# Block turns by VectorE for four of sixteen attention units in a four-layer graph kernel

## The chip, the cores and the metric

The kernel runs on one core of one Trainium2 chip. The metric is the time of one execution on the device in microseconds. TensorE multiplies matrices and turns (transposes) tiles, VectorE and ScalarE work on rows, GpSimd does slower elementwise work, and SP (SyncE) only issues DMAs, one after the other, in the order of its program.

## The reference

Four graph layers run one behind the other on N = 4096 nodes with 128 features; `adj` is a dense 4096x4096 f32 matrix in which a zero means "no edge".

```
L0: msg = relu((adj @ x) @ W_msg.T + b);  x1 = layernorm(GRU(msg, x))
L1: x2 = layernorm(D^-1/2 (adj + I) D^-1/2 (x1 @ W) + b + x1)
L2: q, k, v = x2 @ Wq + bq, ...  (4 heads of 32)
    a = q k^T / sqrt(32), -inf where adj == 0;  alpha = softmax(a)
    out = alpha @ v;  r = x2 @ Ws + bs
    x3 = layernorm(beta * r + (1 - beta) * out + x2)
L3: xt = logmap(mobius(x3 @ W_h.T, bias));  y = layernorm(relu(...(adj @ xt)) + x3)
```

The layer norms and the residual sums are as the kernel's steps show them. All results are f32.

## The kernel before

**Layers 0, 1 and 3** multiply columns of `adj` from a ring of eight slots of 1 MB (`product`, L437; loads at L328 and L409) with a stationary operand, in eight chunks of 512 nodes. `stat_x` and `stat_s` hold the stationary tiles; `stat_s` is written by layer 0, read by layer 1, and its tiles are written again, chunk by chunk, for layer 3 by GpSimd's step `xt` (L1463).

**Layer 2, the attention,** is the stage that the change touches. Each of the 8 chunks has 4 row tiles of 128 nodes. The 4096 key nodes of a row tile are cut into 4 columns of 1024 (`BLOCK`), so a chunk has 16 columns. Two columns make a set, so a chunk has 8 sets. A set is worked off in 16 units (`UPS`) of 128 key nodes and a chunk has 128 units, also called places: every engine writes its instructions out in a loop over k = 0 to 127, and the constants say at which k something is done. Nothing but semaphores keeps the engines together.

- TensorE, `scores` (L541): at every even place, the scores of one head and one column ahead of time (two products of 512), `SCORE_LEAD` = 13 of these ahead, into two pairs of PSUM banks used in turn. It may not run more than two ahead of VectorE's masks.
- VectorE, `mask` (L1096): at every odd place, adds the mask, keeps the row minimum, and writes 128x1024 into `cols` (two sets deep, L226).
- ScalarE, `exponent` (L803): for one head of one set, a 128x2048 exp in place in `cols`, four a set, `EXP_LEAD` = 4 ahead, at the places in `EXP_PLACES`.
- TensorE, `turn_unit` (L573): for each unit, four 128x128 transposes (one a head) of `cols` into one of three PSUM banks (`TurnBanks`).
- The copy of a turned unit into SBUF, `turned[k % 8]`, by VectorE (43 of 128, L1115) or ScalarE (85 of 128, L810). The eight slots are pieces of `arena` (L227); slots 6 and 7 are stages 10 and 11.
- TensorE, `attend` (L584): four products of a turned unit with the values, summed in bank 7. They come in batches of four, `ATTEND_LAG` = 7 places behind: at places 3, 7, 11 and 15 of a set it attends four units, at place 11 units 4 to 7 of the set, at place 3 units 12 to 15 of the set ahead of it.
- GpSimd, `mask_bias` (L1353): turns two halves of an `adj` block (128x512 each) into a bf16 mask, column by column, `BIAS_LEAD` = 6 columns ahead. Between them stand the post steps of the chunk before (L1363 to L1467), and once a row tile the six small steps of `block_mix` (L1469).
- SP (L340 to L405): mask loads into two 128x512 buffers, each as soon as GpSimd has read what lay there; queries once a row tile; residuals and the store of x3 once a chunk. Then the ring loads of layer 3 follow in the same queue, the first four slots when the second to last set is turned, the others when the last one is.

## Time and profile before

| | us |
|---|---|
| median of 3 runs (least, most) | 1860.52 (1857.96, 1862.22) |
| the profiled execution's own time | 1859.99 |
| its span in the trace | 1858.3 |
| busy: TensorE matmul | 1805.1 |
| busy: TensorE weight load | 1215.9 |
| busy: VectorE | 1229.1 |
| busy: ScalarE | 983.0 |
| busy: GpSimd | 925.3 |

Matmuls are pipelined and their ends are modelled, so a TensorE that shows as busy is not thereby at its peak. The attention stage runs from about 600 to 1611 us of the span. PE is TensorE, PEld its weight load, DVE is VectorE, ACT is ScalarE, POOL is GpSimd, SPq is SP's queue of DMA issues.

### The profile page before, as it was taken

The numbers are of one execution on the slowest core, as the hardware profiler recorded it, in microseconds if no ns is written. First come the engines' busy times: TensorE is split into PE (matmuls) and PEld (weight loads), VectorE is DVE, ScalarE is ACT, GpSimd is POOL, SyncE is SP. The second block draws the span as 40 slices with busy tenths as digits, with TensorE's granted clock in tenths as the row PEclk, the third lists the DMA queues.
The fourth block names the chain that finished last, engine by engine and source line by source line (L and its number), as shares of the span: only waits on it lengthen the run. The fifth ranks groups of instructions, "written<-read, shape, count | busy, mean of one in ns | idle before, by whom it ended". The sixth has DMA issues, their size and how long they took to land.

```text
span 1858.3 us, 41304 instructions
## 1 busy us (share of the span) xinstructions
PE 1805.1 (97%) x15504; PEld 1215.9 (65%) x15504; DVE 1229.1 (66%) x2398; ACT 983.0 (53%) x1512; POOL 925.3 (50%) x981
## 2 busy tenths in 40 slices
PE   7999999999996999999999999999999999999996
PEld 3444444444444888888888888888888888644442
DVE  4777775122226888898888888888988889401322
ACT  0111110101004888888888888988888988501101
POOL 0111111111225756778788788787787886540211
PEclk9999999999997999999999999999999999999998
DMA  9867767799977322213222222232133231697781
GB/s 376 303 227 260 256 225 251 270 391 380 400 271 220 93 91 72 83 58 95 88 73 90 74 82 86 70 92 91 60 93 93 64 96 49 242 356 281 281 325 71
DMA packets 110305, 328.82 MB, mean 177 GB/s; under 512 B 13104, under 2 KB 31280, under 8 KB 85552
## 3 DMA queue, kind: packets, MB, share of 16 engines
q1 hardware_dynamic: 87552, 285.25, 43.9%
q10 hardware_dynamic: 20016, 32.78, 4.9%
q0 software_dynamic: 2560, 8.39, 1.6%
q8 instruction: 115, 1.88, 0.4%
q14 instruction: 62, 0.51, 0.1%
HBM read 299.11 MB, written 27.26 MB: 176 GB/s over the span
## 4 chain that ended last, share of the span: by engine, by line
PE 59%; issue 3%; ACT 2%; POOL 2%; DVE 1%; POOLq 0%; DVEq 0%; ACTq 0%
PE bank L580 21%; PE bank L553 13%; PE bank L594 13%; PE bank L446 11%; ACT arena L807 2%; POOL arena L1360 1%; DVE arena L1124 1%; PE bank L434 0%; ACT L858 0%; PE bank L622 0%; PE bank L690 0%; POOL small L1480 0%; ACT arena L819 0%; PE bank L602 0%; POOL small L1367 0%
## 5 line engine op out<-in xcount | busy, mean ns | idle before, releaser
L580 PE MATMUL bank<-ident,arena 128*128 128x128 f32 x4096 | 540.0, 274 | 5.4 <-ACT arena L807 2.4
L580 PEld LDWEIGHTS bank<-ident,arena 128*128 128x128 f32 x4096 | 478.1, 141 | 82.5 <-DVE arena L1124 7.7
L807 ACT ACTIVATE arena<-arena,small 128x2048 f32<-128x2048 f32 x256 | 512.5, 2002 | 0.1
L819 ACT ACTIVATE arena<-bank 128x512 f32<-128x512 f32 x680 | 382.4, 596 | 125.3 <-PE bank L580 123.0
L446 PE MATMUL bank<-arena,stat_s 128*128 128x512 f32 x1008 | 441.4, 595 | 2.1 <-issue 1.2
L553 PE MATMUL bank<-k,parts 128*128 128x512 f32 x1024 | 371.8, 445 | 13.3 <-DVE small L1109 7.0
L446 PEld LDWEIGHTS bank<-arena,stat_s 128*128 128x128 f32 x1008 | 190.2, 191 | 228.3 <-issue 226.9
L1124 DVE COPY arena<-bank 128x512 f32<-128x512 f32 x344 | 236.7, 688 | 73.3 <-PE bank L580 71.6
L1360 POOL TENSOR_SCALAR early<-arena 128x512 bf16<-128x512 f32 x128 | 246.3, 1925 | 68.9 <-DVE small L1109 26.7
L594 PE MATMUL bank<-arena,stat_x 128*32 128x128 f32 x8192 | 276.5, 276 | 0.0
L1360 POOL TENSOR_SCALAR arena<-arena 128x512 bf16<-128x512 f32 x128 | 247.2, 1931 | 40.5 <-DVE small L1109 19.8
L446 PE MATMUL bank<-arena,stat_x 128*128 128x512 f32 x512 | 229.2, 599 | 10.7 <-DMA arena<-adj_cols 8.5
L594 PEld LDWEIGHTS bank<-arena,stat_x 128*32 128x32 f32 x8192 | 208.1, 109 | 42.8 <-issue 42.8
L553 PEld LDWEIGHTS bank<-k,parts 128*128 128x128 f32 x1024 | 155.6, 191 | 68.0 <-issue 44.2
L446 PEld LDWEIGHTS bank<-arena,stat_x 128*128 128x128 f32 x512 | 96.4, 192 | 125.7 <-issue 125.4
L1109 DVE CUSTOM_DVE_ANT_0 arena<-bank,early,small 128x1024 f32<-128x1024 f32 x128 | 163.5, 1279 | 16.6 <-issue 9.3
L1109 DVE CUSTOM_DVE_ANT_0 arena<-bank,arena 128x1024 f32<-128x1024 f32 x128 | 155.9, 1219 | 26.2 <-PE bank L580 20.9
L1109 DVE CUSTOM_DVE_ANT_0 arena<-bank,arena,small 128x1024 f32<-128x1024 f32 x128 | 163.2, 1277 | 6.2 <-issue 5.2
L1109 DVE CUSTOM_DVE_ANT_0 arena<-bank,early 128x1024 f32<-128x1024 f32 x128 | 155.8, 1218 | 15.0 <-PE bank L553 7.8
L1305 POOL TENSOR_SCALAR small<-small 128x4 f32<-128x4 f32 x32 | 13.0, 407 | 251.5 <-DVE small L937 251.5
L1367 POOL TENSOR_TENSOR small<-small 128x4 f32<-128x4 f32 x160 | 78.8, 492 | 60.5 <-DVE small L1185 35.8
L1367 POOL TENSOR_TENSOR arena<-arena 128x512 f32<-128x512 f32 x64 | 76.3, 1192 | 36.4 <-ACT arena L848 20.7
(152 smaller groups left out, 1182.8 us busy)
## 6 DMA issues: line engine op xcount, KB each, us to landing
arena<-adj_cols SPq DMA_DIRECT2D x190, 1024.0 KB, 6.3
arena<-adj SPq DMA_DIRECT2D x256, 256.0 KB, 2.7
k_dram<-arena ACTq DMA_DIRECT2D x32, 256.0 KB, 6.7
q_dram<-arena ACTq DMA_DIRECT2D x32, 256.0 KB, 11.7
k<-k_dram POOLq DMA_DIRECT2D x32, 256.0 KB, 8.5
parts<-q_dram SPq DMA_DIRECT2D x128, 64.0 KB, 2.3
x_dram<-arena ACTq DMA_DIRECT2D x16, 256.0 KB, 3.6
arena<-x_dram ACTq DMA_DIRECT2D x16, 256.0 KB, 4.9
```

The lines of the kernel that those rows point to most:

```text
L446: mm_ = pe.matmul(bank[:, to, :], stat[:, jt, :], ring[:, s, j, :], start=(jt == 0), stop=(jt == TILES - 1))
L553: last = pe.matmul(bank[:, u + i, :], parts[:, t % 2, h * P:(h + 1) * P], k4[:, h, at_:at_ + CHUNK], start=True, stop=True)
L580: last = pe.transpose(bank[:, b_, h * P:(h + 1) * P], cols[:, st % SETS, h, u * P:(u + 1) * P], ident[:, :])
L594: last = pe.matmul(bank[h * C:(h + 1) * C, 7, st * P:(st + 1) * P], stat_x[:, k % UPT, h * C:(h + 1) * C], turned[k % TURNED][:, h * P:(h ...
L807: act.activation(cols[:, s_, h, :], cols[:, s_, h, :], ACT.Exp, bias=shift[:, t % 2, 1, i:i + 1], scale=-1.0, accum_out=blocksum[:, t % 2, ...
L819: act.activation(turned[k % TURNED], bank[:, TURN_BANKS.bank(("unit", k)), :], ACT.Copy).then_inc(unit_copied_act, 1)
L1109: dve.tensor_tensor_reduce(out=cols[:, s_, h, hi * BLOCK:(hi + 1) * BLOCK], in0=bank[:, 2 * (h % 2):2 * (h % 2) + 2, :].rearrange("p b n - ...
L1124: dve.tensor_copy(turned[k % TURNED], bank[:, TURN_BANKS.bank(("unit", k)), :]).then_inc(unit_copied_dve, 1)
L1305: step(c, "eps", pool.tensor_scalar(rstd, mean_var[:, :, 1], LN_EPS, None, ALU.add))
L1360: pool.tensor_scalar(maskbias[m % 4][:, e * HALF:(e + 1) * HALF], adj_in[e], 0.0, MASKED, ALU.is_equal, ALU.mult).then_inc(bias_ready, 1)
L1367: step(c, name, pool.tensor_tensor(out_, a, b, op))
```

## The change

Of the 16 units of a set, units 6, 7, 14 and 15 are no longer turned by TensorE. VectorE turns them from `cols` in 32x32 blocks (`turn_blocks`, one instruction over 128x512 a unit), at VectorE's places 0 and 1 (units 6 and 7) and 7 and 9 (units 14 and 15), into `pair_blocks`, which lies in the last eight tiles of `stat_s`. SP stores the pair to DRAM (512 KB, `store_pair`), waits for that, and loads it back (`load_pair`) in four DMAs of 128 KB, with runs of 1 KB, so that the four row blocks change places; the destination `pair_slot` is the two slots 6 and 7 taken together. The attend products of these units read `pair_slot` through a view with runs of 32. Loads wait until the pair that lay in the slots has been attended.

VectorE copies 12 units a chunk in place of 43, and ScalarE 84 in place of 85. Most exps change their place by one to three. SP's program is written out anew: in each column first the mask load of six columns on, then the pair store, then queries or the store of x3 where they are due, then the pair load. GpSimd waits for the last pair store ahead of the step `xt` that writes over `pair_blocks`.

```diff
+BLOCK_TURN_AT = {6: 0, 7: 1, 14: 7, 15: 9}
+PAIRS = ((6, 7), (14, 15))
-VECTOR_PLACES = (2, 5, 9, 12, 15)
-VECTOR_ALSO = (38, 58, 84, 87, 91, 93)
-VECTOR_NOT = (37, 57, 69)
-EXP_MOVED = {37: 38, 57: 58, 65: 66, 69: 71, 89: 88, 93: 94}
+VECTOR_PLACES = ()
+VECTOR_ALSO = (2, 19, 25, 58, 66, 82, 88, 89, 91, 98, 115, 123)
+VECTOR_NOT = ()
+EXP_MOVED = {1: 2, 5: 7, 13: 12, 17: 20, 21: 24, 25: 26, 29: 28, 37: 39, 45: 44, 49: 50, 57: 59, 61: 60, 65: 66, 69: 71, 73: 74, 77: 76, 85: 88, 93: 90, 97: 98, 101: 104, 105: 106, 109: 108, 113: 115, 117: 120, 121: 123, 125: 124}
+MASK_AHEAD = 6
...
+    pair_dram = nc.dram_tensor("pair_dram", [2, P, 2 * CHUNK], F32)
+        pair_slot = arena[:, RING + 10 * CHUNK:RING + 12 * CHUNK]
+        pair_blocks = stat_s[:, TILES - 2 * TPC:TILES, :].rearrange("p t f -> p (t f)")
+        def pair_tiles(ap):
+            return ap.rearrange("p (b u h n) -> p u h b n", b=P // C, u=2, h=H)
...
+            def store_pair(g):
+                i = pairs_until(g)
+                sp.wait_ge(blocks_turned, 2 * (i + 1))
+                if i >= 2:
+                    sp.wait_ge(pair_landed, 16 * (P // C) * (i - 1))
+                sp.dma_start(pair_dram[i % 2, :, :], pair_blocks).then_inc(pair_out, 16)
+            def load_pair(g):
+                i = pairs_until(g)
+                sp.wait_ge(pair_out, 16 * (i + 1))
+                if i == 0:
+                    sp.wait_ge(gcn_x2_out, 16 * CHUNKS)
+                if g + 1 >= TURNED:
+                    sp.wait_ge(unit_used, g + 1 - TURNED + 1)
+                for j in range(P // C):
+                    sp.dma_start(pair_slot[j * C:(j + 1) * C, :].rearrange("k (q n) -> k q n", q=P // C),
+                                 pair_dram[i % 2, :, j * 2 * P:(j + 1) * 2 * P].rearrange("(q k) n -> k q n", q=P // C)
+                                 ).then_inc(pair_landed, 16)
+            def attention_loads(c):
+                for st in range(SPC):
+                    for half_set in range(2):
+                        ahead = c * COLS + 2 * st + half_set + MASK_AHEAD
+                        if ahead < CHUNKS * COLS:
+                            load_mask(ahead // COLS, ahead % COLS, False)
+                        for pair in PAIRS:
+                            if pair[0] // UPB == half_set:
+                                store_pair(c * UPC + st * UPS + pair[0])
+                        if half_set == 1 and st % SETS == 1:
+                            ahead = c * TPC + st // SETS + 2
+                            if ahead < CHUNKS * TPC:
+                                load_queries(ahead // TPC, ahead % TPC, False)
+                        if half_set == 1 and st == 4 and c > 0:
+                            store_x3(c - 1)
+                        for pair in PAIRS:
+                            if pair[0] // UPB == half_set:
+                                load_pair(c * UPC + st * UPS + pair[0])
+                load_residuals(c)
...
+                if is_block_turned(k):
+                    pe.wait_ge(pair_landed, 16 * (P // C) * (pairs_until(c * UPC + k) + 1))
...
-                    turn_unit(c, k, first)
+                    if not is_block_turned(k):
+                        turn_unit(c, k, first)
...
+            def turn_blocks(c, k):
+                st, u = k // UPS, k % UPS
+                i = pairs_until(c * UPC + k)
+                dve.wait_ge(exp_ready, (c * SPC + st) * H + H)
+                if i > 0:
+                    dve.wait_ge(pair_out, 16 * i)
+                dve.transpose(pair_tiles(pair_blocks)[:, in_pair(k), :, :, :],
+                              cols[:, st % SETS, :, u * P:(u + 1) * P].rearrange("p h (j k) -> p h j k", j=P // C)
+                              ).then_inc(blocks_turned, 1)
...
+                    for u, place in BLOCK_TURN_AT.items():
+                        if k % UPS == place:
+                            turn_blocks(c, k - place + u)
```

## Rows read from the trace of the kernel before

**Rows 1.** The page, part 1: busy us, share of the span, instructions.
```profile
PE 1805.1 (97%) x15504; PEld 1215.9 (65%) x15504; DVE 1229.1 (66%) x2398; ACT 983.0 (53%) x1512; POOL 925.3 (50%) x981
```
**Rows 2.** The page, part 4: shares of the chain by line.
```profile
PE bank L580 21%; PE bank L553 13%; PE bank L594 13%; PE bank L446 11%; ACT arena L807 2%; POOL arena L1360 1%; DVE arena L1124 1%; PE bank L434 0%; ACT L858 0%; PE bank L622 0%; PE bank L690 0%; POOL small L1480 0%; ACT arena L819 0%; PE b
```
**Rows 3.** The chain in order of time: start us, us, what.
```profile
940.38 1.28 ACT L858
...
1452.59 1.28 ACT L858
```
**Rows 4.** Busy us by engine in seven chunk windows: one, then sum and mean.
```profile
928.70:1056.80 128.10, 127.26 (x1685) 105.81 (x1684) 112.86 (x207) 112.89 (x168) 101.48 (x107) 1.00 0.26 82
...
sum 896.70, PE 892.99 PEld 742.74 DVE 792.08 ACT 789.37 POOL 693.96; mean PE 127.57 PEld 106.11 DVE 113.15 ACT 112.77 POOL 99.14
```
**Rows 5.** TensorE in order of time: start us, us, line, tiles, count.
```profile
1111.48 0.73 PE L553 MATMUL bank<-k,parts 128*128 128x512 f32 x2
1112.06 1.03 PE L580 MATMUL bank<-ident,arena 128*128 128x128 f32 x8
1112.85 0.71 PE L553 MATMUL bank<-k,parts 128*128 128x512 f32 x2
1113.39 1.04 PE L580 MATMUL bank<-ident,arena 128*128 128x128 f32 x8
1114.36 1.08 PE L594 MATMUL bank<-arena,stat_x 128*32 128x128 f32 x32
```
**Rows 6.** Groups of one chunk, 928.6 to 1056.95: busy us, mean ns, idle before.
```profile
L594 PE MATMUL bank<-arena,stat_x 128*32 128x128 f32 x1024 | 34.6, 276 | 0.0
...
L1124 DVE COPY arena<-bank 128x512 f32<-128x512 f32 x43 | 29.6, 688 | 7.7 <-PE bank L580 7.4
...
L1189 DVE TENSOR_REDUCE small<-arena 128x4 f32<-128x512 f32 x1 | 0.7, 682 | 0.0
```
**Rows 7.** VectorE in order of time, the same stretch as rows 5.
```profile
1112.36 1.23 DVE L1109 CUSTOM_DVE_ANT_0 arena<-bank,arena 128x1024 f32<-128x1024 f32 x1
...
1113.51 0.69 DVE L1124 COPY arena<-bank 128x512 f32<-128x512 f32 x1
1114.12 1.22 DVE L1109 CUSTOM_DVE_ANT_0 arena<-bank,arena 128x1024 f32<-128x1024 f32 x1
```
**Rows 8.** The 256 KB stores of x3, L379, in the attention stage.
```profile
DMA to landing us min/median/max: 3.2/3.4/4.7
```
**Rows 9.** The mask loads of 256 KB, L345, in the attention stage.
```profile
DMA to landing us min/median/max: 2.5/2.7/4.6
```
**Rows 10.** The ring loads of 1 MB, L328, over the span.
```profile
DMA to landing us min/median/max: 4.7/6.1/23.6
```
**Rows 11.** SP's queue in order of time: four query loads of 64 KB.
```profile
986.22 2.18 SPq L354 DMA_DIRECT2D parts<-q_dram  x4
```
**Rows 12.** The page, part 6: KB each, median us to landing.
```profile
parts<-q_dram SPq DMA_DIRECT2D x128, 64.0 KB, 2.3
```
**Rows 13.** GpSimd in order of time: the bias operations of four columns.
```profile
931.89 3.94 POOL L1360 TENSOR_SCALAR arena<-arena 128x512 bf16<-128x512 f32 x2 [0.25 <-POOL small L1367]
...
941.55 3.95 POOL L1360 TENSOR_SCALAR arena<-arena 128x512 bf16<-128x512 f32 x2 [0.25 <-POOL small L1367]
...
952.06 3.94 POOL L1360 TENSOR_SCALAR early<-arena 128x512 bf16<-128x512 f32 x2 [0.25 <-POOL small L1367]
...
961.15 3.92 POOL L1360 TENSOR_SCALAR early<-arena 128x512 bf16<-128x512 f32 x2 [0.25 <-POOL arena L1367]
```
**Rows 14.** Who waited for whom, 928.6 to 1056.9: us in total, times, longest.
```profile
ACT small L857 <- POOL small L1367: 1.1, 1, 1.1
```
**Rows 15.** SP's queue, then TensorE, at the end of the attention stage.
```profile
1596.74 15.60 SPq L328 DMA_DIRECT2D arena<-adj_cols  x8
...
1598.18 2.02 PE L580 MATMUL bank<-ident,arena 128*128 128x128 f32 x16 [0.46 <-ACT arena L819]
...
1610.93 3.70 PE L446 MATMUL bank<-arena,stat_s 128*128 128x512 f32 x8
```

More of the change, by code:

```diff
@@ L100, in __call__, with is_block_turned, pe_turns, pairs_until @@
         return c * len(self.names) + self.names.index(name) + 1
+def is_block_turned(k):
+    return k % UPS in BLOCK_TURN_AT
+PE_UNITS = [k for k in range(UPC) if not is_block_turned(k)]
+def pe_turns(g):
+    return g // UPC * len(PE_UNITS) + sum(k < g % UPC for k in PE_UNITS)
+def pairs_until(g):
+    return g // UPS * len(PAIRS) + sum(pair[-1] < g % UPS for pair in PAIRS)
+def block_turns(g):
+    return g // UPS * len(BLOCK_TURN_AT) + sum(u < g % UPS for u in BLOCK_TURN_AT)
+def in_pair(k):
+    return [pair.index(k % UPS) for pair in PAIRS if k % UPS in pair][0]
 class TurnBanks:
@@ L111, in __init__ @@
         for k in range(UPC):
-            self.uses.append(("unit", k))
+            if not is_block_turned(k):
+                self.uses.append(("unit", k))
             if k % UPT == OUT_AT:
@@ L141 @@
 LAST_BLOCK_CHUNK = CHUNKS - BLOCK // CHUNK
-BY_VECTOR = [k for k in range(UPC) if (k % 16 in VECTOR_PLACES or k in VECTOR_ALSO) and k not in VECTOR_NOT]
-BY_SCALAR = [k for k in range(UPC) if k not in BY_VECTOR]
+BY_VECTOR = [k for k in PE_UNITS if (k % 16 in VECTOR_PLACES or k in VECTOR_ALSO) and k not in VECTOR_NOT]
+BY_SCALAR = [k for k in PE_UNITS if k not in BY_VECTOR]
 EXP_PLACES = [EXP_MOVED.get(k, k) for k in range(1, UPC, 4)]
```

68 lines of the change are left out of this document (33 added, 35 removed).

## The prediction

> **What bounds the kernel now.** I read the page's engine shares first. TensorE is busy 97% of the span [rows 1], but every engine works in every stage, so I went on to the chain of waits: it consists of TensorE lines, with the turns of L580 first at 21% of the span [rows 2]. The change touches only the attention stage. One chain piece, the reload of ScalarE's table behind the tanh (L858), comes once a chunk, and two of its occurrences, four chunks apart, give (1452.59 - 940.38) / 4 = 128.05 us a chunk, 128.1 below [rows 3]. Over seven such windows the means are TensorE 127.6, VectorE 113.2, ScalarE 112.8 and GpSimd 99.1 us, and DMA engines are busy a quarter of the time at 82 GB/s [rows 4]. So TensorE ends each chunk, yet VectorE and ScalarE have only 15 us of room in 128. The granted clock is 1.00 (the 2.4 GHz level) throughout. This is what the reader is to see: a cheaper TensorE gains at most until the next engine, 14 us further on.
>
> **Turns removed from TensorE.** Four of the 16 units of a set are no longer turned there, 2 pairs in each of 64 sets, 128 pairs. In TensorE's timeline eight turns (two units) start at 1112.06 and the next scores at 1112.85, 0.79 us; the eight in front of an attend batch run from 1113.39 to 1114.36, 0.97 us [rows 5]. The removed units 6, 7, 14, 15 are of the second sort, but the small gap ahead of the attend batch may stay. I take 0.85 us: 128 x 0.85 = **-109 us** (bounds -101 and -124), or 16.0 - 1.7 = 14.3 us a set and 114.5 a chunk. The attend products stay the same in number; they read 32-element runs at a stride, for which no row exists: 0 taken, up to 5% of their 34.6 us a chunk [rows 6], 1.7 us, as the far end; below nothing I see no way.
>
> **VectorE.** It loses 43 - 12 = 31 copies a chunk and gains 32 block turns. A copy of 128x512 out of PSUM is listed at 688 ns [rows 6], but in the timeline it starts at 1113.51 and the next mask at 1114.12: it takes 0.61 us of the engine [rows 7]. VectorE without them is 113.2 - 31 x 0.61 = 94.3 us. The trace has no VectorE transpose. Nearest rows: this copy (0.61), a reduction over 128x512 from SBUF, 682 ns [rows 6], and as the far end a mask operation over twice the elements, 1.22 to 1.28 us [rows 7]. I take 0.65: 94.3 + 20.8 = 115.1 us, as much as TensorE. At 0.61 it is 113.8, at 1.28 it is 135.3.
>
> In the Trainium skill, "VectorE: DVE Perf Modes", section "The three transpose paths", a 128x128 bf16 block turn takes 311 ns, and "Vector Engine (DVE) Microarchitecture Reference", section "The reshape front-end and per-opcode configuration", has one element per cycle and lane. No run here shows either. An estimate by them for 512 elements is 0.7 us, and the chunk would be held at 94.3 + 22.4 = 116.7 us by VectorE, still under the time forecast below.
>
> **ScalarE** copies 84 units a chunk in place of 85: 112.8 - 0.6 = 112.2 us. The other places for exps and copies move waits only; no instruction is added. I cost them at nothing: TensorE's three turn banks cover a move of one or two places, and where that cover fails one copy or exp, 0.6 to 2.0 us, shows.
>
> **The new wait: block turn, store, load, attend.** Unit 6 is turned at VectorE's place 0, unit 7 at place 1, behind that place's mask, and the mask stands behind TensorE's scores of place 0. In the trace scores start at 1111.48 and 1112.85, their masks at 1112.36 and 1114.12 [rows 5, 7]: 0.9 to 1.3 us, and up to 1.8 when VectorE is fuller, which it will be. Add a mask (1.26) and a block turn (0.65): turned 2.8 to 3.7 us behind TensorE's place 0. The store of 512 KB: one of 256 KB takes 3.4 us at the median [rows 8]; by the least times of the 256 KB and 1 MB loads, 2.5 and 4.7 us, 768 KB more cost 2.2 us [rows 9, 10], so 256 KB more cost 0.7: 4.1 us. Then four loads of 128 KB: four issues of 64 KB take SP 2.18 us [rows 11] and each lands 2.3 us after its own issue [rows 12]; the last is issued some 1.5 us behind the first, so 1.5 + 2.3 + 0.1 for the double size = 3.9 us. Together 10.8 to 11.7 us. TensorE reaches the attend of unit 6 at place 11, 4.0 + 3.15 + 3.1 + 0.5 = 10.75 us after place 0 (places 0-3 with all turns, 4-7 without two, 8-11 up to the batch, and units 4 and 5), and from there it has 3.55 us to the set's end. The store stands in series with the load, and nothing else hides them. A late pair delays place 11, which lies behind the start of the next pair's path at place 8, so it costs once a set, not twice: the set becomes 14.35 to 15.25 us against 14.3. I take the middle, 14.8: 64 x 0.5 = **+32 us** (3 to 61). The units 12 to 15 behind it on TensorE, and ScalarE, which waits for turned units, stand still with it. The pairs move 128 x 1 MB, 17 MB a chunk, some 140 GB/s more, so the DMA share goes from 0.26 to about 0.7: transfers may land later, none earlier.
>
> The Trainium skill, "DMA: Bandwidth & Descriptors", section "Anatomy of one DMA", gives 2.0 us plus bytes at 436 GB/s, most of the fixed part the write receipt. By that rule each half of the trip is an estimated 3.2 us, the pair is in time and this term is zero. The store row, 3.4 us for half the bytes [rows 8], is longer than the rule's 2.6, so the sum keeps the row.
>
> **SP's order and GpSimd.** SP's program was: mask load as soon as the mask buffer is free. Now each column holds mask load, pair store, wait for that store, pair load, in this order. SP is at the mask load again only after the four pair issues, about 9.4 us behind the column's start, which is 2 us into the next column. From the mask load to the next one: 0.35 for the second issue, 2.7 landing [rows 9], 3.94 for the two bias operations [rows 13], together 7.0 of a column's 7.2 to 7.4 us. So GpSimd's post steps, (99.1 - 16 x 3.94) / 16 = 2.3 us a column on average, fit only into the landing time. Between the biases of four successive columns stand more: 941.55 - 935.83 = 5.7, 952.06 - 945.50 = 6.6, 961.15 - 956.00 = 5.2 us [rows 13]. There the store is held back, and GpSimd's results reach ScalarE later. ScalarE already waited 1.1 us for the tanh's argument in before [rows 14]. Bias 16, which stands ahead of that argument, ended at 935.83 [rows 13], 4.5 us ahead of the table reload at 940.38 [rows 3]; the new order puts it some 2 to 3 us later against the places, and every place behind comes sooner. I take 4 us a chunk for this wait and the smaller ones like it (between 0, if GpSimd's slack absorbs it, and 8, two waits of 4): 8 x 4 = **+32 us** (0 to 64). Behind a held ScalarE stand the copies, and TensorE is out of turn banks after three places.
>
> **The end.** The ring loads of the last layer stood at 1596.74 in SP's queue, TensorE's last set of turns began at 1598.18 and the first product at 1610.93, with no wait [rows 15]. Now they are queued behind the last pair load. The last set has no scores to fill with: exps done, turn 1.3, store 4.1, load 3.9, attend 1, second load 3.9, attend 1 = 15.2 us against 12.8; and the first ring slot, issued some 3 us before that end, lands 4.7 us later [rows 10]. **+4 us** (2 to 8). The last layer is TensorE's alone, so it is not given back. GpSimd's new wait for the last store costs nothing: only the last chunk's prepared rows stand behind it, and they are read by a product a whole column later. In the first set nothing is late but the pair itself, under 1 us.
>
> **Sum** against the profiled execution, 1860.0 us (1858.3 span; the median of the runs is 1860.5, 0.5 above): -109 + 32 + 32 + 4 = -41, **1819 us**, 122.4 us a chunk.
>
> **Rivals.**
> A, the pair is in time and GpSimd's slack absorbs the order: the three engines at 112 to 115 us hold the chunk, with 2 us for queueing, 117: -109 + 16 + 4 = -89, **1771 us**. For it: the low ends of the path (10.8 against 10.75). By the skill's DMA rule above this is the case to expect. Against it: three engines without room, 1.1 us already waited.
> B, slower: VectorE's block turn is dear. It decides from (128.1 - 94.3) / 32 = 1.06 us each; at the far end of 1.28 the chunk is 135.3: 8 x 7.2 = +57, **1917 us**. Against it: every one-input row moves an element per pass.
> C, slower: SP's chain sets the column. Mask load, landing, both biases and the 2.3 us of post steps in full series make 9.3 us a column; it costs more than the turns saved from 8.0 us on. With a third of the way there, 8.25 us a column and 132 a chunk, +31 us, **1891 us**. For it: 7.0 of 7.2 us are already serial. Against it: post steps fit under landings in most columns.
> D, the waits just cancel the turns: within a few us of 1860.
>
> **Numbers.** Forecast 0.50, A 0.26, B 0.07, C 0.12, D 0.05. The forecast's own range by its terms is 1785 to 1855; the range given, 1766 to 1876, takes in A and the near side of C. A difference of 0.2% (3.7 us) is what the measurement can tell from none. Faster 0.76 (the forecast and A), same 0.05, slower 0.19.
>
> **What the trace after would show.** L580 down to 3072 turns and no busier each. The block turn near 0.65 us (over 1.06: B). TensorE's wait on a landing of the pair slot ahead of L594, about 0.5 us on average per set (none: A). The store near 4.1 us, the last load 3.9 behind the first issue. ScalarE's wait for GpSimd at the tanh 3 to 5 us a chunk. SP's pair store starting late behind the mask load (in most columns: C). A chunk at 122 us. Wrong if chunk time stands at VectorE's busy time, or if the loss lies in another engine's wait than these.

## The result and the profile after

The change makes the kernel slower: 1927.9 us (1926.6 to 1934.1) against 1860.7 in the same comparison, ratio 1.037 (95% interval 1.035 to 1.039). The forecast was 1819 us with a range of 1766 to 1876, so the sign, the size and the range are all wrong. The profiled execution took 1926.6 us with a span of 1924.9, 66.6 us more than before.

The page of the kernel after, part 1; it answers to [rows 1]:

```profile
PE 1737.6 (90%) x14480; PEld 1109.6 (58%) x14480; DVE 1232.3 (64%) x2406; ACT 983.0 (51%) x1504; POOL 925.5 (48%) x981
```

TensorE has 67.5 us less work and 66.6 us more span: 134 us of new idle time. The next view answers to [rows 4]: seven windows of one chunk each, here cut where a chunk's first attend products start. One chunk, then sum and mean.

```profile
1008.80:1144.50 135.70, 119.81 (x1561) 94.18 (x1564) 113.65 (x207) 113.25 (x168) 101.86 (x106) 0.96 0.62 200
...
sum 952.80, PE 832.31 PEld 648.48 DVE 790.35 ACT 789.20 POOL 682.64; mean PE 118.90 PEld 92.64 DVE 112.91 ACT 112.74 POOL 97.52
```

A chunk takes 136.1 us where it took 128.1. From the first attend of the first chunk to that of the last it is 952.8 us against 894.7, +58. The last chunk adds 3.8 us and what lies behind the attention 3.9; 0.8 arose before it. No engine fills the chunk: VectorE, ScalarE and GpSimd have the work they had. The DMA share rose from 0.26 to 0.62. The groups of that chunk, which answer to [rows 6] (busy us, mean ns, idle before):

```profile
L645 PE MATMUL bank<-ident,arena 128*128 128x128 f32 x384 | 51.6, 279 | 0.5 <-DVE arena L1226 0.5
...
L667 PE MATMUL bank<-arena,stat_x 128*32 128x128 f32 x1028 | 38.4, 283 | 14.7 <-DMA arena<-pair_dram 14.7
...
L1206 DVE STREAM_TRANSPOSE stat_s<-arena 128x512 f32<-128x512 f32 x32 | 22.6, 706 | 2.9 <-DMA pair_dram<-stat_s 2.9
```

The turns are down to 384 a chunk, 3072 in all. The attend (L667) waits 14.7 us a chunk for the landing of a pair. TensorE's timeline beside [rows 5] shows how, with the wait in front of each instruction in brackets:

```profile
1111.79 0.64 PE L667 MATMUL bank<-arena,stat_x 128*32 128x128 f32 x16
1113.83 0.64 PE L667 MATMUL bank<-arena,stat_x 128*32 128x128 f32 x16 [1.40 <-DMA arena<-pair_dram]
...
1120.28 0.64 PE L667 MATMUL bank<-arena,stat_x 128*32 128x128 f32 x16
1124.62 1.08 PE L667 MATMUL bank<-arena,stat_x 128*32 128x128 f32 x16 [3.69 <-DMA arena<-pair_dram]
1125.62 1.22 PE L618 MATMUL bank<-k,parts 128*128 128x512 f32 x2
1126.65 1.54 PE L645 MATMUL bank<-ident,arena 128*128 128x128 f32 x8
```

Both pairs are late, 11 us apart. Behind the long stop the same eight turns take 1.54 us in place of 1.03. The granted clock of these stretches (the number behind the busy time and the count), on TensorE:

```profile
1120.00:1124.60 4.60, 0.93 (x20) 0.96 0.58 175
1124.60:1128.00 3.40, 3.38 (x27) 0.55 0.68 229
1128.00:1132.00 4.00, 4.00 (x53) 1.00 0.46 141
```

After 3.69 us of standing still TensorE works at 0.55, near the 1.2 GHz level, for some 3.4 us, then at 2.4 GHz again. So a wait for a pair can cost more than its length. Not each does: of the seven stops of 3 us or more on TensorE between 605 and 1660 us, six are followed by 3.4 us at 0.50 to 0.72 and one by 3.4 us at 1.00; behind the 24 stops of 1.0 to 1.5 us it is 1.00 every time. In the seven chunks the clock is 0.96 to 0.99; in before it was 1.00.

Where the late pair comes from is in SP's queue (start, duration) and, below it, in GpSimd's timeline:

```profile
1108.99 2.46 SPq L417 DMA_DIRECT2D arena<-pair_dram  x4
1113.12 2.35 SPq L387 DMA_DIRECT2D arena<-adj  x2
1115.57 0.38 SPq L406 DMA_DIRECT2D pair_dram<-stat_s  x1
1119.52 2.54 SPq L417 DMA_DIRECT2D arena<-pair_dram  x4
```

```profile
1104.67 0.23 POOL L1458 TENSOR_SCALAR small<-small 128x4 f32<-128x4 f32 x1
...
1111.16 3.94 POOL L1447 TENSOR_SCALAR early<-arena 128x512 bf16<-128x512 f32 x2 [0.25 <-POOL small L1454]
```

VectorE's timeline of the same pair:

```profile
1111.26 0.70 DVE L1206 STREAM_TRANSPOSE stat_s<-arena 128x512 f32<-128x512 f32 x1
1111.89 1.19 DVE L1182 CUSTOM_DVE_ANT_0 arena<-bank,arena 128x1024 f32<-128x1024 f32 x1
```

The pair was turned at about 1111.97. Its store went out at 1115.57, 3.6 us later: in front of it in SP's program stand two mask loads, the first of which waits for GpSimd's bias operation, and GpSimd had been at post steps from 1104.67 until 1111.16. The store then lands after 3.95 us, the four loads are issued, and the attend starts at 1124.62. So the late pair is no single slow step but a row of four in one queue. Over 600 to 1700 us, who waited for whom (us in total, times, longest), the engines first, then SP's queue:

```profile
PEld bank L667 <- DMA arena<-pair_dram: 148.0, 101, 5.5
PE bank L667 <- DMA arena<-pair_dram: 120.8, 91, 5.3
...
DVE stat_s L1206 <- DMA pair_dram<-stat_s: 29.9, 23, 4.1
```

```profile
SPq L417 <- DMA pair_dram<-stat_s: 287.6, 125, 5.3
SPq L415 <- PE bank L667: 102.0, 81, 2.7
SPq L406 <- DVE stat_s L1206: 87.9, 70, 3.2
SPq L387 <- POOL early L1447: 44.1, 44, 2.4
SPq L387 <- POOL arena L1447: 37.5, 50, 2.3
```

SP is blocked on four different things in turn (GpSimd's biases make two rows), and each holds up all that stand behind. Averaged over the middle of the stage, a column of SP's queue is 2.02 us from the first mask issue to the store, 4.18 until the store has landed, 1.97 for the four load issues and 0.31 to the next mask issue: 8.48 us, the whole of a column. Part 6 of the page (KB each, median us to landing), beside [rows 9, 12]:

```profile
arena<-adj SPq DMA_DIRECT2D x256, 256.0 KB, 3.6
pair_dram<-stat_s SPq DMA_DIRECT2D x128, 512.0 KB, 4.0
arena<-pair_dram SPq DMA_DIRECT2D x512, 128.0 KB, 2.8
```

Mask loads land in 3.6 us where they took 2.7.

Averages over the fifth to the 112th of the 128 pairs, from the timelines, show the trip link by link (the 0.02 to 0.07 us between the store's landing and the first load's issue have no row of their own):

| | forecast | after | e5, no masks | e20, masks of 64 KB |
|---|---|---|---|---|
| turned to store issued | 0 | 0.58 | 0.03 | 0.70 |
| store to landing | 4.1 | 4.17 | 2.92 | 3.03 |
| four issues | 1.5 | 1.50 | 1.49 | 1.45 |
| last load to landing | 2.4 | 3.19 | 3.15 | 3.16 |
| landing to attend | 0 | 0.17 | 0.63 | 0.32 |
| turned to attend | 8.0 | 9.62 | 8.29 | 8.68 |

### The profile page after: what moved, and what is told of

Read it like the earlier page. It is cut to its first block and busy times, and to the rows that moved or that the text cites. A ratio compares the mean times of both kernels' runs of the same rounds, so it can differ in the third digit from the quotient of the medians.

```text
span 1924.9 us, 40211 instructions
## 1 busy us (share of the span) xinstructions
PE 1737.6 (90%) x14480; PEld 1109.6 (58%) x14480; DVE 1232.3 (64%) x2406; ACT 983.0 (51%) x1504; POOL 925.5 (48%) x981
## 5 line engine op out<-in xcount | busy, mean ns | idle before, releaser
L891 ACT ACTIVATE arena<-bank 128x512 f32<-128x512 f32 x672 | 369.3, 599 | 165.8 <-PE bank L645 165.2
L645 PE MATMUL bank<-ident,arena 128*128 128x128 f32 x3072 | 411.8, 278 | 8.0 <-DVE arena L1226 4.3
L667 PE MATMUL bank<-arena,stat_x 128*32 128x128 f32 x8192 | 303.8, 281 | 121.1 <-DMA arena<-pair_dram 120.8
L645 PEld LDWEIGHTS bank<-ident,arena 128*128 128x128 f32 x3072 | 366.8, 143 | 67.2 <-DVE arena L1226 7.6
L618 PE MATMUL bank<-k,parts 128*128 128x512 f32 x1024 | 380.5, 454 | 13.9 <-DVE small L1182 7.6
L667 PEld LDWEIGHTS bank<-arena,stat_x 128*32 128x32 f32 x8192 | 206.3, 111 | 211.9 <-DMA arena<-pair_dram 148.0
L1206 DVE STREAM_TRANSPOSE stat_s<-arena 128x512 f32<-128x512 f32 x256 | 180.6, 706 | 32.8 <-DMA pair_dram<-stat_s 29.9
L1454 POOL TENSOR_TENSOR arena<-arena 128x512 f32<-128x512 f32 x64 | 76.1, 1189 | 20.0 <-ACT arena L920 10.3
```

Of the source, the lines that this page charges most:

```text
L618: last = pe.matmul(bank[:, u + i, :], parts[:, t % 2, h * P:(h + 1) * P], k4[:, h, at_:at_ + CHUNK], start=True, stop=True)
L645: last = pe.transpose(bank[:, b_, h * P:(h + 1) * P], cols[:, st % SETS, h, u * P:(u + 1) * P], ident[:, :])
L667: last = pe.matmul(to, stat_x[:, k % UPT, h * C:(h + 1) * C], weights, start=(u == 0), stop=(u == UPS - 1))
L891: act.activation(turned[k % TURNED], bank[:, TURN_BANKS.bank(("unit", k)), :], ACT.Copy).then_inc(unit_copied_act, 1)
L1206: dve.transpose(pair_tiles(pair_blocks)[:, in_pair(k), :, :, :], cols[:, st % SETS, :, u * P:(u + 1) * P].rearrange("p h (j k) -> p h j k" ...
L1454: step(c, name, pool.tensor_tensor(out_, a, b, op))
```

## The experiments

Four theories were held against each other. T: the trip's length alone, by TensorE's wait for the pair. S: SP's serial chain (mask issues, store, its landing, four issues) sets the column whoever waits. M: mask loads that wait for GpSimd ("the handshake" below) hold up the store in SP's queue. Q: the mask loads' bytes, issued just ahead of the store, make it land later. Ratios are to the kernel before, medians in us.

**e1_const_units** leaves TensorE's wait for the pair out; the attend of these units reads the identity in place of the pair slot, and SP waits for the pair before to have landed.

```diff
-                    pe.wait_ge(pair_landed, 16 * (P // C) * (pairs_until(c * UPC + k) + 1))
-                        weights = pair_tiles(pair_slot)[:, in_pair(k), h, :, :]
+                        weights = ident[:, :].rearrange("p (b n) -> p b n", n=C)
```

> Leaves out the use of the block-turned units: their attend products read a constant 128x128 tile through the same view, so TensorE does not wait for the loads; turns, stores, loads and SP's order all stay. Theory T (the round trip of a pair, 13.1 us from TensorE's place 0 to the attend against 10.75 without a wait, holds every set, and TensorE's clock falls after each stop): the waits of 1.07 us a pair and the clock loss of some 4 us a chunk go, chunk 136 -> 117 us, time 1927 -> 1775 us. Rival S (SP's order holds GpSimd's masks and post steps, 7.0 us serial of every column): chunk stays at 128 or above, time 1860 or more. Rival V (strided attend reads or the block turns themselves are dear): chunk 125 or above, 1835 or more.

Measured 1936.9, ratio 1.041 (1.039 to 1.043): no faster, as S had it (1860 or more) and far from T's 1775. TensorE has no more pair waits, but VectorE now stands in front of its block turn, since the block buffer is free only when the store has landed:

```profile
DVE stat_s L1208 <- DMA pair_dram<-stat_s: 135.3, 77, 4.2
```

T alone falls. The loop closes at 17.0 us a set, as in the kernel after, over SP: 1.72 us from the first mask issue to the store, 4.6 for its landing, 1.85 for four issues and 0.32 to the next mask issue make a column of 8.5 us (S). The wait that this run adds to SP's program holds it for 50.6 us in the stage, so e1 is not quite the kernel after without TensorE's wait; e6 has the same added wait and is much faster, so the wait by itself doesn't set the time.

**e2_no_trip** leaves out stores and loads of pairs as well; the block turns stay.

```diff
-                                store_pair(c * UPC + st * UPS + pair[0])
-                                load_pair(c * UPC + st * UPS + pair[0])
```

> Leaves out the stores and loads of the pairs altogether (the attend products of those units read a constant tile); SP's queue holds mask loads, queries and residuals alone. Theory T: little below the run with the trip kept and not waited for, 1765 to 1775 us, because the traffic and SP's order cost 0 to 1 us a chunk when nobody waits for the pair. Rival S: 60 us or more below that run.

Measured 1818.0, ratio 0.977 (0.975 to 0.980), 124.2 us a chunk: 119 us below e1, as S had it, and 43 above T's upper bound. With the trip left out and the mask loads kept, the change gives -43 us. The stretch 720 to 1400 us, then the waits in it:

```profile
720.00:1400.00 680.00, 637.58 (x8522) 508.57 (x8520) 616.15 (x1139) 613.70 (x910) 554.20 (x569) 0.98 0.28 84
```

```profile
PEld bank L612 <- DVE small L1176: 29.6, 28, 4.0
...
ACT small L918 <- POOL small L1452: 24.4, 5, 5.1
...
DVE small L996 <- POOL arena L1448: 16.2, 5, 4.1
```

TensorE is busy 637.6 of 680, 116.5 us a chunk; 7.8 us a chunk are waits. ScalarE waits 4.9 us once a chunk for GpSimd's post steps, at the logarithm of place 83 (L918). The 1.1 us of [rows 14] stood at the tanh, eight places further on.

**e3_store_first** puts the pair store ahead of the mask loads of its column.

```diff
+                                store_pair(c * UPC + st * UPS + pair[0])
                         ahead = c * COLS + 2 * st + half_set + MASK_AHEAD
                         if ahead < CHUNKS * COLS:
                             load_mask(ahead // COLS, ahead % COLS, False)
```

> Pair store ahead of the mask load in each column. In the changed kernel the store is issued 0.57 us late on average (0.03 at the median, up to 3.6 where SP waits for GpSimd). Theory T, once a set: 64 x 2 stores late by 0.57, but a late pair counts once a set, so 0.6 to 1.1 us a set less, 1927 -> 1860 to 1890 us. Rival L (only the DMAs' own times count, the mask load then shares the store's time): within 10 us of 1927.

Measured 1934.9, ratio 1.041 (1.038 to 1.043), within rival L's 10 us of 1927. The store goes out in time (0.08) and lands in 3.32 us, but the loads now stand behind the masks: 0.76 us later, and the last lands in 3.63 in place of 3.19. Turned to attend is 9.70 us against 9.62. The cost moves from one link to the next.

**e4_order_alone** takes SP's new program without any block turn; places and turns are those of before.

```diff
+BLOCK_TURN_AT = {}
+PAIRS = ()
+VECTOR_PLACES = (2, 5, 9, 12, 15)
```

> The new program of SP without any block turn: all units turned by TensorE, copies and exps at the places of the kernel before. Theory T: the order alone costs nothing, 1858 to 1866 us. Rival S: 1890 us or more.

Measured 1859.2, ratio 0.9993 (0.998 to 1.000), 128.1 us a chunk, as T had it. The order by itself costs nothing.

**e5_one_mask** leaves out all mask loads but the first; the trip is made and waited for.

```diff
+                if not (fresh and m == 0):
+                    return
```

> The changed kernel without the mask loads (all columns use the first column's mask; SP's queue holds the pairs, queries and residuals, GpSimd computes every mask but waits for no load). The pair is still stored, loaded and waited for. Theory M (SP's one queue closes a loop: mask load, 3.6 us landing, 3.94 us of GpSimd, next mask load, and store and load of the pair stand between them): a set falls from 17.0 to 15.4 to 16.0 us, time 1927 -> 1825 to 1860 us. Theory T (the pair's own round trip of 13 us holds the set at 16.6 or more, whatever the masks do): 1900 us or more.

Measured 1823.7, ratio 0.980 (0.978 to 0.982). The whole trip is still there, and the kernel is 104 us faster than after, just below M's range; T is out. The store lands in 2.92 us. M and Q both allow this, since the waits and the bytes are gone together.

**e6_one_mask_const** is e5 with e1's attend.

```diff
+                if not (fresh and m == 0):
+                    return
+                        weights = ident[:, :].rearrange("p (b n) -> p b n", n=C)
```

> As the run without mask loads, and the attend products of block-turned units read a constant tile, so TensorE waits for no pair either; stores and loads of the pairs still run, and VectorE still waits for the store ahead of its next block turn. Theory M: as without any trip, 15.4 us a set, 1815 to 1825 us. Theory T: the same here. If the set stays near 17 us, it is a third thing, store plus load issues in SP's queue (6.7 us a column) or the traffic.

Measured 1809.9, ratio 0.972 (0.970 to 0.974): 5 us below the expected range. Without masks in the queue, waiting for the trip costs 14 us, where trip and masks together cost 110. The kernel is also 8 us faster than e2, although it makes all the stores and loads that e2 leaves out. So the mask loads, or GpSimd's waits for them, are worth at least 8 us of e2's time.

**e7_early** turns the first pair at places -2 and -1 of its set, the second at 6 and 7, and orders SP as load, next store, mask.

```diff
+BLOCK_TURN_AT = {6: -2, 7: -1, 14: 6, 15: 7}
```

> Computes the reference. Units 6 and 7 are turned two places before their set (places 14 and 15 of the set ahead), units 14 and 15 at places 6 and 7; SP's order in each column becomes pair load, next pair's store, mask load, so that neither waits behind a mask. Theory T: about 2 us more lead for one pair and a trip off the set's path, the set 15.5 to 16 us, time 1830 to 1860. Theory M: the masks still stand in the same queue behind a load that waits for TensorE, so GpSimd's masks stay late, 1880 or more.

Measured 2145.8, ratio 1.153 (1.151 to 1.155), the worst of all; only theory M's "1880 or more" holds. SP waits for turns, with the masks behind, and GpSimd for the masks:

```profile
SPq L406 <- DVE stat_s L1205: 385.1, 102, 13.5
```

```profile
POOL early L1449 <- DMA arena<-adj: 110.6, 16, 12.2
...
POOL arena L1449 <- DMA arena<-adj: 90.6, 29, 6.8
```

The pair itself is hardly waited for on TensorE (10.3 us). The run changes the start of the trips and SP's order at once, so it doesn't tell which of them does the harm; together they don't help while everything stands in one queue.

**e8_one_pair** turns only units 14 and 15 in blocks, at places 0 and 1, with before's exp places.

```diff
+BLOCK_TURN_AT = {14: 0, 15: 1}
+PAIRS = ((14, 15),)
+VECTOR_PLACES = (2, 5, 9)
```

> Computes the reference. One pair a set (units 14 and 15), turned at VectorE's places 0 and 1 and attended 18 places later; units 6 and 7 go back to TensorE; VectorE copies 24 units a chunk, ScalarE 88; exps at the places of the kernel before. TensorE's own work is 128.1 - 6.8 = 121.3 us a chunk, VectorE's 119, and the trip has 8 us of slack. Theories T and M both expect faster than the kernel before: 1815 to 1845 us. If SP's queue holds even with one pair, 1860 or more.

Measured 1882.2, ratio 1.0105 (1.009 to 1.012). Half the turns saved, still slower, and 37 us above the range of both theories; TensorE hardly waits for pairs. The exps aren't always done when VectorE comes to the block turn (23.1 us of waits), and SP waits 204 us for the slot of units 6 and 7, which this pair uses too.

**e9_more_mask_buffers** gives the masks a second pair of buffers for columns 6 to 71, so that a mask load waits for an older bias.

```diff
+            return n % 2 if 6 <= n < 72 else 0
+                    sp.dma_start(adj_in[mask_set(n) * 2 + e], adj[bass.ds((c * TPC + t) * P, P),
```

> Computes the reference. The changed kernel, but columns 6 to 71 (to the middle of chunk 4) have a second pair of mask buffers in tiles of stat_s that are free until then, so a mask load waits for the bias of two columns before. Theory M (loop of mask load, landing, GpSimd, with the pair's store and load between): chunks 1 to 3 fall from 136 to 123 to 127 us, chunks 5 and 6 stay at 136, time 1875 to 1890 us. Rival Q (DMA traffic of masks and pairs together, not the waits): all chunks stay at 136.

Measured 1916.9, ratio 1.031 (1.029 to 1.032). SP waits 54 us for GpSimd in place of 82, over the same 600 to 1700 us, but the store still lands in 4.30 us. Where the second pair of buffers is in use, chunks 1 to 3 (counted from 0) take 131.6 us on average against 136.8 in the kernel after; behind it, chunks 5 and 6 take 136.1 against 135.3. So M's direction is there, at half the size or less that was expected. **e11_three_halves** does the like over the whole stage with three half buffers and masks five ahead.

```diff
+MASK_AHEAD = 5
+        adj_in = [stages[4], stages[5], stages[9]]
```

> Computes the reference. Three mask half buffers in rotation in place of two (the mask itself has three buffers in place of four, and masks are made five columns ahead), so SP never waits for the second half of a bias and the loop is 2 us shorter. Theory M: the column falls from 8.5 to about 7.9 us, 1840 to 1880 us. Rival Q: 1915 or more.

Measured 1910.2, ratio 1.027 (1.025 to 1.028), landing 4.22: between the two expectations. Less waiting for GpSimd is worth 11 us over half of the stage (e9) and 18 over all of it.

**e10_traffic** has no mask loads, and in their places transfers of the same size from `adj` to DRAM for which nobody waits. **e15_quarter_traffic** is e10 with 64 KB in place of 256 KB in each.

```diff
+                        sp.dma_start(unused_dram[(c * COLS + m) * 2 + e, :, :],
+                                     adj[bass.ds((c * TPC + t) * P, P),
+                                         b * BLOCK + e * HALF:b * BLOCK + (e + 1) * HALF]).then_inc(unused_out, 16)
+                        continue
```

> As the run without mask loads, but SP issues a DMA of the same 256 KB of adj at each of their places, into an unused region of DRAM, and nobody waits for it; all columns use the first mask. Theory M: the traffic costs a few us, 1825 to 1845 us. Rival Q: 1900 us or more.

> As e10 (the masks are not loaded or waited for, and a stand-in transfer is issued at each place where a mask load was), but each stand-in moves 64 KB instead of 256 KB. The count and the places of the issues are the same. If the bytes ahead of the pair store in the DMA queues lengthen its landing: the landing falls from 4.55 us towards e5's 2.92, and the kernel to 1825 to 1850 us. If it is the issues and the order in the queue whatever their size: landing stays above 4 us and the kernel at 1880 to 1900 us.

e10: 1899.8, ratio 1.022 (1.020 to 1.024), where Q had 1900 or more and M at most 1845. e15: 1823.2, ratio 0.980 (0.978 to 0.983), 2 us below what "by the bytes" had expected. The same issues at the same places; only the bytes differ, and with them the store's landing (part 6, e10 then e15):

```profile
pair_dram<-stat_s SPq DMA_DIRECT2D x128, 512.0 KB, 4.5
...
unused_dram<-adj SPq DMA_DIRECT2D x254, 256.0 KB, 3.8
```

```profile
pair_dram<-stat_s SPq DMA_DIRECT2D x128, 512.0 KB, 2.8
...
unused_dram<-adj SPq DMA_DIRECT2D x254, 64.0 KB, 2.6
```

That is Q: 77 us by bytes, and the issues cost nothing (e15 equals e5).

**e20_quarter_masks** is the fourth corner: the kernel after with all its waits, but mask loads that bring 128 of 512 columns.

```diff
+                    width = HALF if fresh and m < 2 else P
+                    sp.dma_start(adj_in[e][:, 0:width], adj[bass.ds((c * TPC + t) * P, P),
```

> The changed kernel with every wait and every issue, but each mask load brings 128 of its 512 columns (64 KB); the other columns keep what the first load left. With stand-in transfers the bytes were worth 77 us (e10 to e15), the handshake with GpSimd 28 us (changed kernel to e10). If both add up: 1851 us, a store landing of about 3.0 us, below the time before. If the handshake matters more once the landing is short, because a mask load that waits for GpSimd is then the longest link: 1860 to 1880 us. If the stand-ins overstate the bytes since they also write to DRAM: above 1880 us, with the landing near 3.5.

Measured 1860.9, ratio 1.001 (0.999 to 1.002), the low edge of the second expectation: the handshake costs more (38 us) once the landing is short. Its part 6:

```profile
pair_dram<-stat_s SPq DMA_DIRECT2D x128, 512.0 KB, 2.8
...
arena<-adj SPq DMA_DIRECT2D x252, 64.0 KB, 2.6
```

| us | masks wait for GpSimd | nobody waits |
|---|---|---|
| 256 KB each | 1927.9 (after) | 1899.8 (e10) |
| 64 KB each | 1860.9 (e20) | 1823.2 (e15) |

Bytes are worth 67 to 77 us, the handshake (M) 28 to 38.

**e12_masks_by_gpsimd** issues the mask loads from GpSimd's queue, each behind its bias.

```diff
+                        pool.wait_ge(bias_ready, n * 2 - 1 + e)
+                        pool.dma_start(adj_in[e], adj[n // BLOCKS * P:(n // BLOCKS + 1) * P,
```

> Computes the reference. GpSimd issues the mask loads from its own queue, each right behind the bias that frees the buffer; SP's queue holds pairs, queries, residuals. An issue takes GpSimd 0.55 us in the trace of before, 32 a chunk: GpSimd 101.8 + 18 = 120 us a chunk. Theory M: the pair is no longer held behind masks, but GpSimd is full: chunk 125 to 132 us, 1840 to 1895 us.

Measured 1997.1, ratio 1.074 (1.072 to 1.076), 147 us a chunk. SP is rid of the masks and the store lands in 3.2 us (median), but GpSimd, which had 99 us of work a chunk, now has

```profile
720.00:1400.00 680.00, 562.49 (x7237) 440.34 (x7239) 526.89 (x967) 525.33 (x773) 552.93 (x617) 0.94 0.60 187
```

553 of 680 us, 120 a chunk, and its results come too late: from 600 to 1620 us ScalarE waits 57.5 us for its post steps. TensorE still waits 69.0 us for pairs. The run is 100 us above the expected range.

**e14_one_pair_later** is e8 with the turns and VectorE's copies at later places.

```diff
+BLOCK_TURN_AT = {14: 4, 15: 6}
+VECTOR_PLACES = (2, 9, 12)
```

> One pair a set (units 14 and 15), turned by VectorE at places 4 and 6 of the set instead of 0 and 1, so that the exps are done when VectorE comes; the exp places are those of before. The pair has eleven places from its first turn to its attend. Theory that the loss lies in the length of the trip: with half the trips (64 instead of 128) and time for each, TensorE keeps the 54 us of 64 x 0.85, less what the coupling of the engines takes back in the kernel without any trip (there 66 of 109 us, so here up to 33): 1805 to 1840 us, most likely 1830. VectorE's wait for the exp (15 us in e8) is gone. Rival, the store held in SP's queue behind a mask load that waits for GpSimd: it comes in one column of two here and costs nothing as long as the pair has slack; if it decides nevertheless, the time stays near e8's 1882.

Measured 1882.2, ratio 1.011 (1.009 to 1.014): 42 us above the range, at the time that the rival named, but not by its wait. TensorE waits only 2.4 us for pairs, but SP stands in front of the store until VectorE has turned, with the masks behind it:

```profile
SPq L406 <- DVE stat_s L1205: 349.3, 63, 9.5
```

```profile
POOL early L1446 <- DMA arena<-adj: 89.7, 37, 5.4
```

**e18_store_second** moves that store behind the second mask load of the set; **e17_before_places** also takes before's places of copies, with the turns at 4 and 7.

```diff
-                        if half_set == 0:
-                            store_pair(c * UPC + st * UPS + PAIRS[0][0])
+                        if half_set == 1:
+                            store_pair(c * UPC + st * UPS + PAIRS[0][0])
                             load_pair(c * UPC + st * UPS + PAIRS[0][0])
```

> As e14, but the store of the pair stands in SP's program behind the second mask load of the set instead of ahead of it, directly in front of the pair's load. The turns are done before it comes up, so SP does not stand in front of it (349 us in e14), and the mask loads go out as soon as their buffer is free. Theory that SP held by a blocked store delays the masks and through GpSimd's bias VectorE and TensorE: GpSimd's waits for mask loads fall from 120 to below 50 us and the kernel from 1882 to 1845 to 1865 us. Rival, that e14 is slow because neighbouring places leave the copies to ScalarE in a row behind an exp (TensorE waits 110 us for them): the time stays within 8 us of 1882.

> As e18, and VectorE copies at the places of the kernel before (2, 5, 9, 12 of each set and its exceptions, without 15), with the pair's blocks turned at places 4 and 7: VectorE has 34 copies and 16 block turns a chunk, 117 us, ScalarE 78 copies, some 109 us, TensorE 121.8. If ScalarE's copies in a row are what holds TensorE in e14: below e18 by 8 to 25 us, 1835 to 1850 us. If it is SP alone, or VectorE at 117 us gives back what ScalarE gains: within 6 us of e18.

e18: 1905.4, ratio 1.025 (1.023 to 1.028); e17: 1901.3, ratio 1.022 (1.019 to 1.024). e18 missed both of its expectations, the nearer by 15 us. e17 is 4 us from e18, its second expectation, and 51 above its first. In e18 the store now has mask and query loads ahead of it. SP's queue, then TensorE:

```profile
1113.23 2.33 SPq L387 DMA_DIRECT2D arena<-adj  x2
1115.60 1.85 SPq L396 DMA_DIRECT2D parts<-q_dram  x4
1117.56 0.38 SPq L406 DMA_DIRECT2D pair_dram<-stat_s  x1
1123.20 1.73 SPq L417 DMA_DIRECT2D arena<-pair_dram  x4
```

```profile
1128.18 1.08 PE L664 MATMUL bank<-arena,stat_x 128*32 128x128 f32 x16 [5.25 <-DMA arena<-pair_dram]
```

From store to first load issue 5.6 us, then a stop of 5.25 us, which fits Q. SP's wait for turns is gone (9.5 us in e18), yet GpSimd's waits for masks stay (126 us against 120). In its place SP stands before the pair's load: 150 us for TensorE to free the slot and 69 for the store. What holds e8 and e14 at 1882 is not shown: e18 takes away SP's wait for the turns and e17 the rows of copies on ScalarE, both with a later store, and neither is faster.

**e16_later_steps** is e2 with two ScalarE steps that read GpSimd's results moved to later places; like e2, its kernel reads the identity.

```diff
-                return {29: beta_exp, X3_AT + 1: copy_x3, MX_AT + 1: copy_mx, 83: lambda: logs("xn_min"),
-                        91: arg_tanh, logs_at: lambda: logs("pn")}
+                return {29: beta_exp, X3_AT + 1: copy_x3, MX_AT + 1: copy_mx, 86: lambda: logs("xn_min"),
+                        98: arg_tanh, logs_at: lambda: logs("pn")}
```

> As e2 (no stores and loads of pairs; the attend reads what is in the slot), with two of ScalarE's steps that wait for GpSimd moved later: the logarithm of the minimum from place 83 to 86, the tanh argument from 91 to 98. If waits of ScalarE for GpSimd make the kernel without a trip slow (29.2 us of such waits in six and a half chunks of e2), the chunk falls from 124.2 by 2 to 4 us and the kernel from 1818 to 1790 to 1803 us. Rival, the three engines with 113 to 116 us of work a chunk wait for each other anyhow, and GpSimd's late steps only take the place of other waits: within 5 us of 1818, and ScalarE's wait for GpSimd below 10 us in the trace.

Measured 1829.0, ratio 0.983 (0.981 to 0.985), 11 us slower than e2, outside both expectations. Most of the wait stays, 3.9 us a chunk after 4.9:

```profile
L918 ACT ACTIVATE small<-small 128x4 f32<-128x4 f32 x10 | 2.1, 206 | 19.6 <-POOL small L1452 19.6
```

What keeps e2 at 124.2 us a chunk is thus not settled.

## Why the prediction was wrong

Two steps of the sum failed. The turns were counted in full as time, and the trip was priced as if nothing stood ahead of it in SP's queue. By the medians the miss is about 108 us: 66 in the first step, 42 in the second together with SP's order and the end. With the measured value in the first step alone the sum would give +25 us, in the second alone +1; measured are +67.

**Turns off TensorE, -109 us: right in work, wrong as time.** The page has 67.5 us less TensorE work where 109 were forecast; part of the gap may be lower clock. In e2, which pays for no trip, TensorE's work is 116.5 us a chunk (forecast 114.5), 11.1 less than in before, but the chunk falls by 3.9 only, and the kernel by 43 us in place of 109. With TensorE, VectorE and ScalarE all at 112 to 117 us of work, the chunk doesn't run at the longest of them. The sum put these waits of nearly full engines for each other at nothing; only rival A had 2 us a chunk for them. If the 32 us for GpSimd's late results are counted here, for which ScalarE's 4.9 us a chunk in e2 speak, the forecast for e2 is 1787 us and 31 of the 66 remain.

**VectorE 115.1, ScalarE 112.2 us: right within 1.5.** 113.7 and 113.3 in the chunk shown. A block turn is listed at 706 ns and frees the engine after 0.63 us (1111.26 to 1111.89 above; forecast 0.65). Rival B is out. The attend's strided read costs little at most: 283 ns a product against 276 [rows 6], at the lower clock.

**The trip, +32 us: too cheap, and priced alone.** The path from place 0 (or 8, for the second pair) to the attend is 13.1 us on average, forecast 10.8 to 11.7, available 10.75. "Turned" at 3.4 to 3.5 us was inside 2.8 to 3.7, and the store's 4.17 was 4.1 as forecast. The overrun is 0.8 in the last load's landing, 0.6 in the held store, and 0.4 in small rest. It costs once a set, as argued, but 13.1 + 3.55 = 16.6 us instead of 14.8; measured are 17.0, and the clock behind the stops may be the rest. Against e2's 15.5 us a set that is 1.5 us, and by the medians the trip with its masks costs 110 us, where the three terms of cost had 68. I had priced each transfer by rows in which it stood alone or nearly so; the store of 4.1 us was right by luck. Without mask loads it lands in 2.9 us (e5); with 512 KB of masks issued just ahead it needs 4.2. The loads went the other way: their half of the trip takes 1.5 + 3.15 = 4.6 us even in e5, forecast 3.9. In e5 the pair is nearly in time, and e5 costs 14 us more than e6.

By the rule of the Trainium skill ("DMA: Bandwidth & Descriptors", section "Anatomy of one DMA — SWDGE (gpsimd) path") each half of the trip was an estimated 3.2 us. The section's title gives the rule for DMAs that GpSimd issues; these are SP's. The store is near it when no masks are loaded (2.9), and neither the store behind masks (4.2) nor the loads (4.6) are.

**SP's order and GpSimd, +32 us: wrong place.** SP's order by itself is free (e4), and the wait of 3 to 5 us a chunk that I expected at ScalarE's tanh is not there: e2 has 4.9 us at the logarithm ahead of it, and after, with its longer chunk, has neither. What the order does cost appears only together with the trip: the mask load's wait for GpSimd and its bytes lie in front of the store, 28 to 38 and 67 to 77 us. The forecast named the first ("the store is held back") and put a price on GpSimd's results instead of on the pair; it did not see the second. I had written that "transfers may land later, none earlier" and then given this no term, and here bytes cost the most.

**The end, +4 us: inside its bounds, near the far one.** From the last set's first turns to the last layer's first product it is 20.3 us (1657.20 to 1677.51) against 12.8 [rows 15], +7.6 of at most 8. It is in two waits on TensorE, the first still in the last chunk, the second behind the attention:

```profile
1673.06 0.64 PE L667 MATMUL bank<-arena,stat_x 128*32 128x128 f32 x16 [4.04 <-DMA arena<-pair_dram]
1677.51 5.21 PE L511 MATMUL bank<-arena,stat_s 128*128 128x512 f32 x8 [3.81 <-DMA arena<-adj_cols]
```

**Rivals.** A is out by the 120.8 us of pair waits. C, SP's chain sets the column from 8.0 us, is the nearest: a column takes 8.5 us, and e1 shows that the chain would close there even if TensorE never waited. It was given 8.25 us, which is half and not a third of the way from 7.2 to 9.3, and 12%. The range "by its terms", 1785 to 1855, is narrower than the terms' own bounds, which add up to 1741 to 1892. C's chain was mask load, biases, post steps; the one found is mask issues, store, landing, four issues, beside the loop over TensorE's wait for the pair. Two loops of about the same length were each priced alone: removing one uncovers the other.

The clock was no part of the forecast: most of the longer stops are followed by a stretch at a granted clock of 0.50 to 0.72. TensorE's work is 118.9 us a chunk in after against 116.5 in e2 for the same products, some 19 us over eight chunks, if all of that is clock.

Open: the floor of e2, what holds e8 and e14, and whether the masks' bytes delay the store in the shared queue or in the DMA engines and memory. The stand-in transfers went through the same queue as the masks. In e12 the full masks go through GpSimd's queue and the store lands in 3.2 us (median) against 4.0, but there they are also issued at other moments and the chunk is longer. A version of one pair with its transfers in a queue of its own, and a transfer without the round trip through DRAM, weren't tried. Of the kernels that compute everything, none beats the one before, and only e4, which turns no blocks, equals it.

## What to carry to other kernels

When a change puts a store, its landing and a load in series, write down for each link what stands ahead of it in its queue, in bytes as well as in waits: a transfer's landing time in a trace holds for the traffic it had there. SP works off its program in order, and when it serves two loops they are tied together: moving the turns or one DMA to another place moved the waits and didn't remove them (e3, e7, e14, e18). And before paying for work to be moved off the busiest engine, measure what it gives with the new cost left out (e2): here it was 43 us where the sum had 109, too little to pay for 128 trips.

## What the runs showed of the hardware

- The same 512 KB store lands after 2.8 us (median) with 64 KB transfers ahead of it in SP's queue and after 4.5 us with 256 KB ones (e15, e10), at a DMA share of 0.54 and 0.66: on average a third or more of the DMA engines' time was free.
- A 32x32 block turn of 128x512 f32 from SBUF to SBUF takes VectorE 0.63 us, like a copy out of PSUM (0.61 in [rows 7]).
- A stop of TensorE of 3.69 us was followed by 3.4 us at a granted clock of 0.55; a stop of 1.40 us (at 1113.83) by 1.00, with eight turns in 1.03 us. Of the seven stops of 3 us or more between 605 and 1660 us, six were followed by 0.50 to 0.72 and one by 1.00.
